# One product with B and one scan for two slots at a time on VectorE, with the states made in place

## The chip, the cores and the metric

The kernel runs on one core of a Trainium2 chip. The metric is the time of one execution on the device in microseconds (us). Smaller is better.

## What is computed

The input `x` is a batch of 16 images of 48 channels and 64x64 pixels, float32. Two layers follow one another. Each has a mixing step and a small feed-forward network, both added to the running `x`. The first layer mixes with a 3x3 depthwise convolution of one of four experts; the second with a two-dimensional cosine transform, after which each quarter of the spectrum goes through a selective state-space block ("mamba"), and an inverse transform. The change touches only the recurrence in that block:

```python
delta = softplus(einsum('blr,dr->bld', dt, dt_w) + dt_b)
A = -exp(A_log)
dA = exp(delta[..., None] * A)
dBu = delta[..., None] * Bm[:, :, None, :] * xi[..., None]
def step(h, inp):
    dA_t, dBu_t, C_t = inp
    h = dA_t * h + dBu_t
    return (h, einsum('bds,bs->bd', h, C_t))
h0 = zeros((B, d_inner, D_STATE))
_, ys = scan(step, h0, (dA, dBu, Cm))       # over L = 1024 positions
```

There are 96 inner channels with 16 states each, so 1536 recurrences of length 1024 for every image and quarter.

## The kernel before, in words

The 16 images go two at a time through `pair(p)`, eight times. A pair has 8 **units** (2 images times 4 quarters, `UNITS`), and a unit has 12 **slots** (`G`): a slot holds 8 channels x 16 states on the 128 partitions, and 1024 positions along the row (`L`). So there are 96 slots in a pair and 768 in the run. The stretch of a pair in which they are worked off is called the scan stage here. `scan_stage` walks through units `v` and slots `m` on every engine; each engine has its own program in that order, and they meet only at semaphores.

What is done for one slot, by engine:

- **SyncE** spreads 8 rows of delta from memory over the 128 partitions into `dbc` (line 461; a ring of 3).
- **ScalarE** makes the decay `da = exp(delta * A)` from it (`decay`, line 1240; a ring of `DAS` = 3 slots). It may overwrite a ring slot when the scan three slots back is done.
- **TensorE** spreads delta times input over the states with four matmul records (`broadcast_u`, lines 834 and 836) into two PSUM banks: banks 2 and 3 for even slots, 4 and 5 for odd ones. It may write a pair of banks when the scan two slots back is done (`h_ready`), because that scan still read them. In program order it stands one slot ahead of VectorE.
- **VectorE** multiplies these banks in place in PSUM by B (`step`, line 1571; this is called the product with B), and then runs the recurrence along the row (line 1576; this is called the scan). The scan reads the decay from the arena in SBUF and the product from PSUM, and writes the states to `hs` in the arena, a ring of `HSS` = 6 slots. `y_acc` says when a ring slot is free.
- **GpSimd** (POOL in the profile) multiplies the states by C, in place in `hs`, both inputs in SBUF (line 1680). Once in a unit it also makes the input of the next unit (line 1667), gates the output of the last one (line 1689), and adds a strip of the next pair's first layer (line 1697). It works in program order.
- **TensorE** sums three slots at a time over the states (`states`, line 857), which raises `y_acc`. Between these it does the projections of the next unit and the convolution of the next pair.

At the end of a stage VectorE makes the last product with C itself (line 1587, both inputs in SBUF).

Outside the scan stage, VectorE and GpSimd meet in the feed-forward stretches: there VectorE converts from SBUF to SBUF (line 1424, a CAST) while GpSimd adds (line 1638).

Everything named `arena` in the profile is one SBUF buffer; `da`, `hs`, `dbc`, B (`bmat`) and C (`cmat`) are parts of it. `ps` is PSUM.

Of the kernel before, what the change touches and what calls it, by code (L numbers as in the profile page):

```python
# [51 lines left out]
DAS = 3  # L52
HSS = 6
# [19 lines left out]
ARENA = 30300  # L73
# [5 lines left out]
def program(nc, a):  # L79
# [9 lines left out]
    with ctx:  # L89
# [43 lines left out]
        st = sb("st", [128, 8, ST])  # L133
        nrm = sb("nrm", [128, 6, ST + 2])
# [34 lines left out]
        yb = cut(R, 2 * CH // 2, F16).rearrange("p (b n) -> p b n", b=2)  # L169
        assert top[0] <= ARENA  # L170

# [94 lines left out]
        xs_zero = sem("xs_zero")  # L266
        xi_ps = sem("xi_ps")
# [124 lines left out]
        def scan_stage(prep, first, step, conv, last, early=lambda slot, v: None):  # L392
# [13 lines left out]
            last()  # L406

# [155 lines left out]
        def _(pe):  # L563
# [141 lines left out]
            def pair(p, last):  # L705
# [113 lines left out]
                def broadcast_u(v, m):  # L819
# [7 lines left out]
                    if v or m >= 2:  # L827
                        pe.wait_ge(h_ready, n - 1)
                    elif m == 0:
                        pe.wait_ge(sz_ready, 2 * p * UNITS + 2)  # L830
                    else:
                        pe.wait_ge(first_b, 2 * p + 2)
# [4 lines left out]
                              start=True, stop=True).then_inc(ubc_ready, 1)  # L837

# [9 lines left out]
                def states(v, r):  # L848
# [6 lines left out]
                    for c in range(2):  # L855
                        for b in range(TRIO):
                            mm = pe.matmul(ps[b * BLK:(b + 1) * BLK, c, :], gather[:, r, :],  # L857
                                           hs[:, (r * TRIO + b) % HSS, c * 512:(c + 1) * 512],
# [12 lines left out]
                def step(v, m):  # L871

                    w, k = after(v, m, 1)
                    if w < UNITS:
                        broadcast_u(w, k)
                    if v == 0 and m == 0:
                        states_first()
# [87 lines left out]
                scan_stage(prep, lambda: broadcast_u(0, 0), step, conv, final)  # L965
# [25 lines left out]
        def _(act):  # L991
# [102 lines left out]
            def rest(p, last):  # L1094
# [139 lines left out]
                def decay(v, m):  # L1234
# [5 lines left out]
                    act.activation(da[:, m % DAS, :], dbc[:, m % DBC, :], ACT.Exp,  # L1240
                                   scale=a_all[:, v // 2, m:m + 1]).then_inc(da_ready, 1)

                def first():
                    decay(0, 0)
                    for c in range(2):
                        first_states(c, 6 + c, first_c_ps, cmat, first_c)
                    for m in range(1, DAS - 1):
# [71 lines left out]
        def _(dve):  # L1319
# [223 lines left out]
            def rest(p, last, linked):  # L1543
# [16 lines left out]

                def step(v, m):
# [7 lines left out]
                    driven = two(2 + 2 * (m % 2))  # L1569
                    dve.wait_ge(ubc_ready, n + 1)  # L1570
                    dve.tensor_tensor(driven, driven, bmat[:, v % 2, :], ALU.mult).then_inc(bu_ready, 1)  # L1571
                    dve.wait_ge(bu_ready, n + 1)
                    dve.wait_ge(da_ready, n + 1)
                    if v or m >= HSS:
                        dve.wait_ge(y_acc, V * GPB + (m - HSS) // TRIO + 1)
                    dve.tensor_tensor_scan(hs[:, m % HSS, :], da[:, m % DAS, :], driven, 0.0,  # L1576
                                           ALU.mult, ALU.add).then_inc(h_ready, 1)
# [262 lines left out]
```

## Time and profile before

| | |
|---|---|
| median of 3 runs (lowest to highest) | 4236.63 us (4227.06 to 4249.97) |
| the execution that was profiled | 4219.27 us |
| its span in the trace | 4217.4 us |
| busy: TensorE, VectorE, ScalarE, GpSimd | 3708.7, 3493.2, 2772.9, 2345.8 us |
| scan stages, first product with B to line 1587 | eight of 337 to 343 us |

The profile is one execution, seen instruction by instruction. Busy time is the sum over an engine; the share of busy time is a mean over stages with different limits. A group of instructions is one line, operation and shape. "Idle before" is the time that the engine stood still just before these instructions, with what ended it. DVE is VectorE, ACT ScalarE, POOL GpSimd, PE TensorE, PEld its weight loads.

### The profile page before, as it was taken

How to read it: one execution, taken by the hardware profiler on the slowest of the kernel's cores; microseconds unless marked ns; L12 is line 12 of the kernel's file. 1: busy time of each engine (PE TensorE's matmuls, PEld its weight loads, DVE VectorE, ACT ScalarE, POOL GpSimd, SP SyncE). 2: the span in 40 equal slices, each digit the busy share in tenths (PEclk: the TensorE clock that was granted, in tenths of full speed). 3: DMA queues.
4: the chain of work that ended last, by engine and by line, in shares of the span. 5: the costliest groups of instructions: out<-in, count | busy, mean ns of one | idle time of the engine just before them, and what ended most of it. 6: DMA issues, size and time to landing. Idle time of an engine off the chain costs nothing.

```text
span 4217.4 us, 41720 instructions
## 1 busy us (share of the span) xinstructions
PE 3708.7 (88%) x14008; PEld 1348.4 (32%) x14008; DVE 3493.2 (83%) x3101; ACT 2772.9 (66%) x3212; POOL 2345.8 (56%) x1092
## 2 busy tenths in 40 slices
PE   6889988899879998899988999889988899878887
PEld 2332234222342223422244222432234322342223
DVE  2379987799778997699976999679987799778997
ACT  2567757777576775677666775767657767576764
POOL 0138762578426874177732787238762477426873
PEclk9999999999999999999999999999999999998878
DMA  1158861698518884288724887268961698507881
GB/s 40 35 144 214 214 166 47 169 220 205 134 51 207 206 220 100 72 215 219 206 63 119 214 209 171 75 146 212 217 167 47 165 220 201 141 18 196 199 204 46
DMA packets 186045, 644.72 MB, mean 153 GB/s; under 512 B 25660, under 2 KB 26600, under 8 KB 182280
## 3 DMA queue, kind: packets, MB, share of 16 engines
q1 hardware_dynamic: 168808, 596.95, 57.9%
q10 hardware_dynamic: 17024, 45.10, 3.5%
q8 instruction: 113, 1.85, 0.2%
q14 instruction: 100, 0.82, 0.1%
HBM read 525.40 MB, written 78.82 MB: 143 GB/s over the span
## 4 chain that ended last, share of the span: by engine, by line
DVE 35%; issue 25%; PE 18%; ACT 13%; DMA 4%; POOL 4%; SPq 0%; DVEq 0%; ACTq 0%; POOLq 0%
DVE ps L1571 15%; DVE arena L1576 13%; PE ps L673 4%; DMA arena<-dl 3%; PE ps L613 3%; PE ps L664 2%; ACT arena L1036 2%; ACT arena L1018 2%; POOL arena L1689 2%; POOL arena L1680 2%; ACT arena L1240 2%; PE ps L692 2%; DVE arena L1424 1%; ACT L1152 1%; ACT arena L1029 1%
## 5 line engine op out<-in xcount | busy, mean ns | idle before, releaser
L1680 POOL TENSOR_TENSOR arena<-arena 128x1024 f32<-128x1024 f32 x760 | 1785.9, 2359 | 704.3 <-DVE arena L1576 704.3
L1576 DVE TENSOR_TENSOR_SCAN arena<-arena,ps 128x1024 f32<-128x1024 f32 x768 | 1756.4, 2287 | 74.6 <-issue 31.6
L1240 ACT ACTIVATE arena<-arena,a_all 128x1024 f32<-128x1024 f32 x768 | 869.8, 1146 | 692.1 <-DMA arena<-dl 541.4
L834 PE MATMUL ps<-arena,spread 32*128 32x512 f32 x1536 | 876.4, 652 | 142.7 <-DVE arena L1576 140.9
L1571 DVE TENSOR_TENSOR ps<-ps,arena 128x1024 f32<-128x1024 f32 x768 | 928.3, 1209 | 57.5 <-PE ps L836 57.2
L836 PE MATMUL ps<-arena,spread 32*128 32x512 f32 x1536 | 869.1, 653 | 0.0
L857 PE MATMUL ps<-arena,gather 128*32 128x512 f32 x3072 | 519.4, 629 | 12.5 <-DVE arena L1587 12.4
L928 PE MATMUL ps<-x 96*96 96x512 f32 x1008 | 499.1, 613 | 26.5 <-ACT arena L1171 26.5
L834 PEld LDWEIGHTS ps<-arena,spread 32*128 32x128 f32 x1536 | 230.1, 186 | 785.9 <-DVE arena L1576 482.8
L1638 POOL TENSOR_TENSOR x<-x,arena 96x512 f32<-96x512 f32 x64 | 113.9, 1780 | 377.1 <-DVE arena L1415 377.1
L993 ACT ACT_TABLE_LOAD x226 | 290.0, 1283 | 24.7 <-DMA wo<-in_wo 20.7
L928 PEld LDWEIGHTS ps<-x 96*96 96x96 f32 x1008 | 142.3, 162 | 350.7 <-issue 350.7
L746 PE MATMUL ps<-arena,w_in 96*96 96x512 f32 x512 | 246.6, 609 | 8.0 <-ACT x L1286 7.8
L613 PE MATMUL ps<-arena,average 96*96 96x512 f32 x400 | 220.7, 634 | 30.7 <-ACT arena L1029 30.3
L1018 ACT ACTIVATE arena<-ps,eps 96x512 f32<-96x512 f32 x200 | 136.7, 684 | 144.3 <-PE ps L613 144.2
L857 PEld LDWEIGHTS ps<-arena,gather 128*32 128x32 f32 x3072 | 104.9, 112 | 384.8 <-issue 299.3
L836 PEld LDWEIGHTS ps<-arena,spread 32*128 32x128 f32 x1536 | 226.7, 186 | 0.0
L1657 POOL MEMSET arena<- 96x6 f32 x8 | 0.8, 103 | 388.3 <-DVE xq L1538 388.3
L1384 DVE TENSOR_TENSOR arena<-ps,arena 96x512 fp8e5<-96x512 f32 x128 | 86.9, 679 | 130.7 <-ACT arena L1023 130.1
L1036 ACT ACTIVATE arena<-ps 128x1536 f16<-128x1536 f32 x128 | 183.7, 1436 | 1.6 <-PE ps L632 1.6
L1638 POOL TENSOR_TENSOR x<-col_all,arena 96x512 f32<-96x512 f32 x64 | 103.6, 1619 | 145.9 <-DVE arena L1415 145.9
L643 PE MATMUL ps<-arena,w 128*96 128x512 fp8e5 x384 | 105.4, 384 | 83.4 <-DVE arena L1376 77.6
(160 smaller groups left out, 4907.8 us busy)
## 6 DMA issues: line engine op xcount, KB each, us to landing
arena<-dl SPq DMA_DIRECT2D x880, 512.0 KB, 6.9
dl<-arena ACTq DMA_DIRECT2D x64, 384.0 KB, 5.9
x<-pn SPq DMA_DIRECT2D x56, 247.5 KB, 10.5
arena<-in_x SPq DMA_DIRECT2D x9, 1536.0 KB, 13.2
arena<-xq SPq DMA_DIRECT2D x64, 192.0 KB, 6.2
arena<-arena ACTq DMA_DIRECT2D x64, 192.0 KB, 7.5
out<-x SPq DMA_DIRECT2D x64, 192.0 KB, 2.1
arena<-xq SPq DMA_DIRECT2D x64, 191.8 KB, 5.5
```

The lines of the kernel that those rows point to most:

```text
L613: pe.matmul(ps[0:R, LN_DEPTH + j % LN_DEPTH, :], average[:], sq[:, j % LN_DEPTH, :], start=True, stop=True).then_inc(averaged, 1)
L746: mm = pe.matmul(ps[0:DI, 6 + c, :], w_in[:, q, j, :], xs[:, i, c * 512 + 2 * j:c * 512 + 2 * j + 512], start=(j == 0), stop=(j == 1))
L834: pe.matmul(ps[:, bank, :], spread[rows[0], r, :], u[rows[0], i, 0:512], start=True, stop=True)
L836: pe.matmul(ps[:, bank + 1, :], spread[rows[1], r, :], u_low[rows[1], i, :], start=True, stop=True).then_inc(ubc_ready, 1)
L857: mm = pe.matmul(ps[b * BLK:(b + 1) * BLK, c, :], gather[:, r, :], hs[:, (r * TRIO + b) % HSS, c * 512:(c + 1) * 512], start=False, stop=( ...
L928: mm = pe.matmul(ps[0:R, 7, :], diag[:, k, :], taps_of(win[:, v % 2], k), start=(k == 0), stop=(k == TAPS - 1), skip_group_check=True)
L993: exp_table = lambda: act.preload_act_table_set("natural_log_exp_and_others")
L1036: act.activation(hf[:, j % 2, :], ps[:, 4:7, :].rearrange("p b n -> p (b n)"), ACT.Copy).then_inc(hf_ready, 1)
L1240: act.activation(da[:, m % DAS, :], dbc[:, m % DBC, :], ACT.Exp, scale=a_all[:, v // 2, m:m + 1]).then_inc(da_ready, 1)
L1571: dve.tensor_tensor(driven, driven, bmat[:, v % 2, :], ALU.mult).then_inc(bu_ready, 1)
L1576: dve.tensor_tensor_scan(hs[:, m % HSS, :], da[:, m % DAS, :], driven, 0.0, ALU.mult, ALU.add).then_inc(h_ready, 1)
L1680: pool.tensor_tensor(product, product, cmat[:, v % 2, :], ALU.mult).then_inc(pr_ready, 1)
```

## The change

VectorE now takes two slots in one instruction. The product with B reads four PSUM banks and writes to two ring slots of `hs`; the scan then reads decay and product, both from the arena, and writes the states over the product. The two slots are one row of 2048 to the scan; so that nothing of the first slot's last state goes into the second, the first decay of each slot is zero, and is written once in a pair by GpSimd: the exponentials then cover positions 1 to 1023. The first two slots of a stage and the last two are still done one at a time. `DAS` goes from 3 to 4, `HSS` from 6 to 8, and two small tables move into the arena, which grows by 1970 columns.

TensorE fills the four banks for two slots together, and no longer waits for the scan (`h_ready`) but for the product with B (`bu_ready`), since the product is what reads PSUM last.

```diff
-DAS = 3
-HSS = 6
+DAS = 4
+HSS = 8
...
+        def one_slot(v, m):
+
+            return (v == 0 and m < 2) or (v == UNITS - 1 and m >= G - 2)
...
                     if v or m >= 2:
-                        pe.wait_ge(h_ready, n - 1)
+                        pe.wait_ge(bu_ready, n - m % 2)
...
+                def first():
+
+                    broadcast_u(0, 0)
+                    broadcast_u(0, 1)
+                    states_first()
...
-                    w, k = after(v, m, 1)
-                    if w < UNITS:
+                    w, k = after(v, m, 2)
+                    if m % 2 == 0 and w < UNITS:
                         broadcast_u(w, k)
-                    if v == 0 and m == 0:
-                        states_first()
+                        broadcast_u(w, k + 1)
...
-                    act.activation(da[:, m % DAS, :], dbc[:, m % DBC, :], ACT.Exp,
+                    act.activation(da[:, m % DAS, 1:L], dbc[:, m % DBC, 1:L], ACT.Exp,
...
+                def scan(v, m, count):
+
+                    V = p * UNITS + v
+                    n = V * G + m
+                    h, d, b = (v * G + m) % HSS, m % DAS, 2 + 2 * (m % 2)
+                    driven = ps[:, b:b + 2 * count, :].rearrange("p (s b) n -> p s (b n)", s=count)
+                    state = hs[:, h:h + count, :]
+                    dve.wait_ge(ubc_ready, n + count)
+                    if v or m + count > HSS:
+                        dve.wait_ge(y_acc, V * GPB + (m + count - 1 - HSS) // TRIO + 1)
+                    dve.tensor_tensor(state, driven,
+                                      bmat[:, v % 2, :].rearrange("p (o n) -> p o n", o=1)
+                                      .broadcast_to([128, count, L]), ALU.mult).then_inc(bu_ready, count)
+                    dve.wait_ge(bu_ready, n + count)
+                    if v == 0 and m == 0:
+                        dve.wait_ge(da_zero, p + 1)
+                    dve.wait_ge(da_ready, n + count)
+                    line = state.rearrange("p s n -> p (s n)")
+                    dve.tensor_tensor_scan(line, da[:, d:d + count, :].rearrange("p s n -> p (s n)"), line, 0.0,
+                                           ALU.mult, ALU.add).then_inc(h_ready, count)
...
-                    driven = two(2 + 2 * (m % 2))
-                    dve.wait_ge(ubc_ready, n + 1)
-                    dve.tensor_tensor(driven, driven, bmat[:, v % 2, :], ALU.mult).then_inc(bu_ready, 1)
-                    dve.wait_ge(bu_ready, n + 1)
-                    dve.wait_ge(da_ready, n + 1)
-                    if v or m >= HSS:
-                        dve.wait_ge(y_acc, V * GPB + (m - HSS) // TRIO + 1)
-                    dve.tensor_tensor_scan(hs[:, m % HSS, :], da[:, m % DAS, :], driven, 0.0,
-                                           ALU.mult, ALU.add).then_inc(h_ready, 1)
+                    if one_slot(v, m) or m % 2 == 0:
+                        scan(v, m, 1 if one_slot(v, m) else 2)
...
                 pool.memset(xs[:, :, 0:PADL], 0.0).then_inc(xs_zero, 1)
+                pool.memset(da[:, :, 0:1], 0.0).then_inc(da_zero, 1)
```

VectorE at the start of a scan stage, in the order of the program. The scan stands there as SCALAR_TENSOR_TENSOR; `arena<-arena,ps` is out from in, and the brackets name the semaphores that it waits for. Before:

```order
L1571 TENSOR_TENSOR ps<-ps,arena 128x1024 [waits ubc_ready,first_b]
L1576 SCALAR_TENSOR_TENSOR arena<-arena,ps 128x1024 [waits da_ready,bu_ready]
L1571 TENSOR_TENSOR ps<-ps,arena 128x1024 [waits ubc_ready]
L1576 SCALAR_TENSOR_TENSOR arena<-arena,ps 128x1024 [waits da_ready,bu_ready]
L1571 TENSOR_TENSOR ps<-ps,arena 128x1024 [waits ubc_ready]
L1576 SCALAR_TENSOR_TENSOR arena<-arena,ps 128x1024 [waits da_ready,bu_ready]
L1571 TENSOR_TENSOR ps<-ps,arena 128x1024 [waits ubc_ready]
L1576 SCALAR_TENSOR_TENSOR arena<-arena,ps 128x1024 [waits da_ready,bu_ready]
```

The same place on VectorE now, slots 0 to 5:

```order
L1582 TENSOR_TENSOR arena<-ps,arena 128x1024 [waits ubc_ready,first_b]
L1590 SCALAR_TENSOR_TENSOR arena<-arena 128x1024 [waits da_ready,da_zero,bu_ready]
L1582 TENSOR_TENSOR arena<-ps,arena 128x1024 [waits ubc_ready]
L1590 SCALAR_TENSOR_TENSOR arena<-arena 128x1024 [waits da_ready,bu_ready]
L1582 TENSOR_TENSOR arena<-ps,arena 128x2048 [waits ubc_ready]
L1590 SCALAR_TENSOR_TENSOR arena<-arena 128x2048 [waits da_ready,bu_ready]
L1582 TENSOR_TENSOR arena<-ps,arena 128x2048 [waits ubc_ready]
L1590 SCALAR_TENSOR_TENSOR arena<-arena 128x2048 [waits da_ready,bu_ready]
```

From the third slot on there is one row of 2048 where there were two of 1024, and the scan's inputs are the arena alone.

TensorE in the first unit of a stage, around its slots 3 to 5 (L834 and L836 spread one slot, L857 sums three slots over the states, L759 is a projection, L928 the convolution). Before:

```order
L834 MATMUL ps<-arena,spread 128x512 [waits h_ready]
L836 MATMUL ps<-arena,spread 128x512
L759 MATMUL ps<-arena,w_dbc 128x512 [waits sz_ready] x2
L834 MATMUL ps<-arena,spread 128x512 [waits h_ready]
L836 MATMUL ps<-arena,spread 128x512
L857 MATMUL ps<-arena,gather 32x512 [waits pr_ready]
L857 MATMUL ps<-arena,gather 32x512 x5
```

The same place on TensorE now (L839 and L841 spread, L868 sums, L764 projects):

```order
L764 MATMUL ps<-arena,w_dbc 128x512 [waits sz_ready] x2
L839 MATMUL ps<-arena,spread 128x512 [waits bu_ready]
L841 MATMUL ps<-arena,spread 128x512
L839 MATMUL ps<-arena,spread 128x512 [waits bu_ready]
L841 MATMUL ps<-arena,spread 128x512
L868 MATMUL ps<-arena,gather 32x512 [waits pr_ready]
L868 MATMUL ps<-arena,gather 32x512 x5
```

Two slots are spread one behind the other, after the product with B of the two slots ahead of them and no longer after a scan; the other matmuls of two slots stand between.

## Rows read from the trace of the kernel before

**Rows 1.** The page, chain of work that ended last, shares of the span by engine.

```profile
DVE 35%; issue 25%; PE 18%; ACT 13%; DMA 4%; POOL 4%; SPq 0%; DVEq 0%; ACTq 0%; POOLq 0%
```

**Rows 2.** Eight scan stages: length, busy us (x instructions) by engine, granted clock, DMA.

```profile
core 0: us, PE busy (x) PEld busy (x) DVE busy (x) ACT busy (x) POOL busy (x), PEclk, DMA share, GB/s
263.30:606.30 343.00, 320.81 (x1132) 91.68 (x1130) 330.11 (x197) 238.11 (x234) 263.79 (x116) 0.99 0.82 202
...
3812.60:4149.90 337.30, 285.70 (x972) 77.67 (x970) 329.96 (x196) 208.56 (x203) 255.18 (x109) 0.84 0.80 192
sum 2728.00, PE 2519.23 PEld 717.20 DVE 2638.52 ACT 1875.14 POOL 2102.02; mean PE 314.90 PEld 89.65 DVE 329.82 ACT 234.39 POOL 262.75
```

**Rows 3.** Timeline of VectorE in a scan stage: start us, us, engine, line, operation.

```profile
338.16 1.21 DVE L1571 TENSOR_TENSOR ps<-ps,arena 128x1024 f32<-128x1024 f32 x1
339.40 2.29 DVE L1576 TENSOR_TENSOR_SCAN arena<-arena,ps 128x1024 f32<-128x1024 f32 x1
341.61 1.21 DVE L1571 TENSOR_TENSOR ps<-ps,arena 128x1024 f32<-128x1024 f32 x1
342.85 2.29 DVE L1576 TENSOR_TENSOR_SCAN arena<-arena,ps 128x1024 f32<-128x1024 f32 x1
```

**Rows 4.** VectorE by line and shape: count, busy us, mean ns, idle before.

```profile
L1576 DVE TENSOR_TENSOR_SCAN arena<-arena,ps 128x1024 f32<-128x1024 f32 x768 | 1756.4, 2287 | 74.6 <-issue 31.6 <-ACT arena L1240 10.3 <-DVE ps L1571 7.5
L1571 DVE TENSOR_TENSOR ps<-ps,arena 128x1024 f32<-128x1024 f32 x768 | 928.3, 1209 | 57.5 <-PE ps L836 57.2
...
L1609 DVE TENSOR_TENSOR x<-x,ps 96x512 f32<-96x512 f32 x64 | 43.7, 683 | 41.3 <-PE ps L673 40.4
...
L1587 DVE TENSOR_TENSOR arena<-arena 128x1024 f32<-128x1024 f32 x8 | 9.8, 1224 | 0.3
...
L1592 DVE TENSOR_TENSOR arena<-ps,arena 96x1024 f32<-96x1024 f32 x8 | 9.8, 1221 | 17.8 <-PE ps L857 17.8
```

**Rows 5.** One line each: duration ns min/median/max, first and last start.

```profile
L1576 DVE TENSOR_TENSOR_SCAN arena<-arena,ps x768: 2286/2287/2289, 265.9 to 4147.6; 128x1024 f32<-128x1024 f32 x192
...
L1680 POOL TENSOR_TENSOR arena<-arena x760: 2332/2357/2398, 268.3 to 4146.5; 128x1024 f32<-128x1024 f32 x190
```

**Rows 6.** Timeline of GpSimd in the same stage, with what ended its idle time.

```profile
320.52 6.97 POOL L1680 TENSOR_TENSOR arena<-arena 128x1024 f32<-128x1024 f32 x3
...
345.22 2.35 POOL L1680 TENSOR_TENSOR arena<-arena 128x1024 f32<-128x1024 f32 x1 [1.08 <-DVE arena L1576]
348.66 2.35 POOL L1680 TENSOR_TENSOR arena<-arena 128x1024 f32<-128x1024 f32 x1 [1.09 <-DVE arena L1576]
```

**Rows 7.** Timelines of VectorE and GpSimd at the ends of two scan stages.

```profile
606.28 1.22 DVE L1587 TENSOR_TENSOR arena<-arena 128x1024 f32<-128x1024 f32 x1
...
606.79 1.85 POOL L1697 TENSOR_TENSOR x<-x 96x512 f32<-96x512 f32 x1 [1.55 <-ACT x L1286]
...
1620.18 1.23 DVE L1587 TENSOR_TENSOR arena<-arena 128x1024 f32<-128x1024 f32 x1
...
1620.70 1.84 POOL L1697 TENSOR_TENSOR x<-x 96x512 f32<-96x512 f32 x1 [1.56 <-ACT x L1286]
...
L1697 POOL TENSOR_TENSOR x<-x x56: 1254/1269/1861, 319.3 to 3647.0; 96x512 f32<-96x512 f32 x56
```

**Rows 8.** Timelines in a feed-forward stretch, and the CAST's shortest, median and longest.

```profile
695.84 1.15 POOL L1638 TENSOR_TENSOR x<-col_all,arena 96x512 f32<-96x512 f32 x1 [1.90 <-DVE arena L1415]
...
696.00 1.81 DVE L1424 CAST arena<-arena 128x1536 fp8e5<-128x1536 f16 x1 [0.24 <-issue]
...
L1424 DVE CAST arena<-arena x128: 943/950/1824, 162.4 to 4209.4; 128x1536 fp8e5<-128x1536 f16 x128
```

**Rows 9.** Timeline of TensorE: one slot spread, and the next matmul behind it.

```profile
349.09 0.69 PE L834 MATMUL ps<-arena,spread 32*128 32x512 f32 x1
349.09 0.69 PE L836 MATMUL ps<-arena,spread 32*128 32x512 f32 x1
349.62 0.59 PE L834 MATMUL ps<-arena,spread 32*128 32x512 f32 x1
349.63 0.59 PE L836 MATMUL ps<-arena,spread 32*128 32x512 f32 x1
350.14 1.96 PE L746 MATMUL ps<-arena,w_in 96*96 96x512 f32 x4
```

More of the change, by code:

```diff
@@ L72 @@
 WIN = (ROWS + 2) * HP
-ARENA = 30300
+ARENA = 32270
 WS = KC + 3
@@ L132, in program @@
         pw_bias = sb("pw_bias", [R, 1])
-        st = sb("st", [128, 8, ST])
-        nrm = sb("nrm", [128, 6, ST + 2])
         x = sb("x", [R, PX])
@@ L169, in program @@
         yb = cut(R, 2 * CH // 2, F16).rearrange("p (b n) -> p b n", b=2)
+        st = cut(128, 8 * ST).rearrange("p (k s) -> p k s", k=8)
+        nrm = cut(128, 6 * (ST + 2)).rearrange("p (k s) -> p k s", k=6)
         assert top[0] <= ARENA
@@ L266, in program @@
         xs_zero = sem("xs_zero")
+        da_zero = sem("da_zero")
         xi_ps = sem("xi_ps")
@@ L857, in states @@
                             mm = pe.matmul(ps[b * BLK:(b + 1) * BLK, c, :], gather[:, r, :],
-                                           hs[:, (r * TRIO + b) % HSS, c * 512:(c + 1) * 512],
+                                           hs[:, (v * G + r * TRIO + b) % HSS, c * 512:(c + 1) * 512],
                                            start=False, stop=(r == GPB - 1), skip_group_check=True)
@@ L963, in final @@
                     project(QUADS - 1, 1, 7)
-                scan_stage(prep, lambda: broadcast_u(0, 0), step, conv, final)
+                scan_stage(prep, first, step, conv, final)
                 pe.wait_ge(mo_copied, (p + 1) * 2 * QUADS)
@@ L1244, in first @@
                     decay(0, 0)
+                    decay(0, 1)
                     for c in range(2):
                         first_states(c, 6 + c, first_c_ps, cmat, first_c)
-                    for m in range(1, DAS - 1):
+                    for m in range(2, DAS - 1):
                         decay(0, m)
@@ L1584, in final @@
                     n = V * G + G - 1
-                    q, i, slot = QUADS - 1, (UNITS - 1) % 2, (G - 1) % HSS
+                    q, i, slot = QUADS - 1, (UNITS - 1) % 2, (UNITS * G - 1) % HSS
                     dve.wait_ge(h_ready, n + 1)
@@ L1678, in step @@
                         pool.wait_ge(h_ready, n + 1)
-                        product = hs[:, m % HSS, :]
+                        product = hs[:, (v * G + m) % HSS, :]
                         pool.tensor_tensor(product, product, cmat[:, v % 2, :],
```

## The prediction, made before the changed kernel ran

> **What bounds the kernel now.** I read the shares of the chain of waits first [rows 1]: VectorE has 35% of it, more than any other engine. Shares over the whole run mix stages, so I read next the table of the eight scan stages [rows 2]. They take 2728 of 4217 us, and in each VectorE is busy for some 330 of 341 us, GpSimd for 264, ScalarE for 238. TensorE shows 321 us, but its records overlap. The timeline of VectorE [rows 3] shows how tight it is: product with B at 338.16, scan at 339.40, next product at 341.61, next scan at 342.85. That is 1.24 + 2.21 = 3.45 us a slot; 96 slots make 331 of the 341 us. So the scan stage is bound by VectorE issuing 2 instructions a slot without a gap, and the other 10 us are its waits [rows 4].
>
> Beside it GpSimd multiplies by C. A product takes 2.36 us, and GpSimd then stands still for 1.08 us until the next scan ends [rows 6]. It runs right through the scans and neither suffers: 768 scans lie between 2286 and 2289 ns, 760 products between 2332 and 2398 [rows 5]. What the two instructions read matters for what follows: the scan has one input in SBUF (the decay) and one in PSUM, GpSimd has both in SBUF.
>
> **The change on VectorE alone.** 92 of the 96 slots of a stage go in 46 instructions of two; 4 stay single. What it saves is the fixed part of an instruction. A product of 512 columns from PSUM to SBUF takes 683 ns, one of 1024 takes 1221 [rows 4], so 512 columns cost 538 and the fixed part is 145 ns. The new product also writes to SBUF, and 2048 columns should take 1221 + 1076 = 2.30 us against 2 x 1.21. For the scan there is one size only: between nothing and the 145 ns are saved, 4.57 or 4.43 us for two slots; I take 4.43, since it is the same engine. With the distances between starts that rows 3 show (0.03 us behind a product, -0.08 behind a scan), two slots go from 6.90 to 2.30 + 0.03 + 4.43 - 0.08 = 6.68 us. That would save 0.22 x 46 x 8 = 81 us.
>
> **The small parts.** GpSimd's extra memset and the new waits on it come once in a pair, in front of the first scan; the columns are four. The exponentials lose one column of 1024. TensorE must now spread two slots in a row, after the product with B. One takes 1.05 us from its start to the next matmul [rows 9], so two take 2.1, plus some 0.8 us until TensorE starts; the scan that runs meanwhile takes 4.43. If that cover were gone, up to 2.9 us a pair of slots would show. Queued behind TensorE's new wait are its sums over the states, its projections and the convolution; who waits for those (ScalarE, and VectorE through `y_acc`) stands two slots or more behind, and the ring has grown to 8. I count all of this at nothing.
>
> **The part that decides: the scan's second input.** The scan now reads its second input from SBUF too, and the trace shows what happens when VectorE and GpSimd both do that. At 606.28 VectorE starts its last product with C, line 1587, both inputs in SBUF. At 606.79, in the middle of it, GpSimd starts line 1697, and takes 1.85 us where its median is 1.27: 0.58 too long, so that it seems to begin at 607.37, 0.13 before VectorE ends at 607.50. At 1620.70 the same again, 1.84 us [rows 7]. The other way round it holds too: GpSimd adds from 695.84 for 1.15 us, undisturbed, and a CAST that VectorE starts at 696.00 takes 1.81 us where the median is 0.95 [rows 8]; it loses 0.86 us and seems to begin 0.13 us before GpSimd ends. So whoever comes second stands still until 0.13 us before the end of the first. Against it stands that line 1587 is a TENSOR_TENSOR and the CAST has one input; no scan with two inputs in SBUF is in the trace.
>
> The Trainium skill has this as a rule ("SBUF — State Buffer", section "Who interferes with whom"): a VectorE instruction with two SBUF inputs reads the second through an interface that it shares with GpSimd, and whichever of the two starts first keeps it for the whole instruction. Rows 7 and 8 agree; for a scan no run here shows it. By that rule the sum is the one that follows, without it the 81 us gain above.
>
> **The sum, if scans and GpSimd exclude each other.** Then neither VectorE's nor GpSimd's chain sets a stage, but both in turn: all of GpSimd's work plus all scans, while the products with B (one SBUF input) run beside GpSimd. Between two scans GpSimd needs 2 x 2.33 us (three in a row took 6.97 [rows 6]), the product with B only 2.30, so it is hidden. For each of the first seven stages:
> - GpSimd's work, by its busy time: 263.8 us [rows 2] (95 products with C, seven each of the three others).
> - Scans: 46 x 4.43 + 4 x 2.29 = 212.9.
> - Hand-over from GpSimd to VectorE, 0.13 us early: -0.13 x 50 = -6.5. The other way I take zero: it could be 0.13 early too, or 0.08 late, as GpSimd starts at 345.22 behind a scan that ended at 345.14 [rows 3, 6].
> - The first product with B, in front of everything: +1.2.
>
> That is 471.4 us where they now take (2728.0 - 337.3) / 7 = 341.5: +129.9 each, +909 for seven. The last stage has 255.2 us on GpSimd: 462.8 against 337.3, +125. Together +1034 us, and 4219.3 + 1034 = 5253. Whether VectorE or GpSimd wins a hand-over hardly matters: if scans go first, GpSimd falls behind, until TensorE's sums (which stand in front of the spreading of later slots) hold VectorE back and GpSimd catches up; one of the two is at work all the time. The saved 0.22 us is in the scans' 4.43, the product's part is hidden.
>
> TensorE stays below that: 321 / 48 = 6.7 us of work for two slots in 9.8. In the last stage its granted clock is 0.84, a mix of the levels of 2.4 and 1.2 GHz, with less to do, and the stage is no longer for it [rows 2]; at that mean 6.7 would be 8.0, still below 9.8.
>
> **Bounds of this case.** Both hand-overs 0.13 early: 50 x 0.13 x 8 = 52 less, 5200. GpSimd always 0.08 late, +32, and one wait of the size of the 1.55 us in rows 7 in each of 64 units, +99: 5380.
>
> The sum is against the profiled execution of 4219.3 us, which is 17 us below the median of the runs, inside their spread. I leave the forecast at **5250 us**.
>
> **Rivals.**
> - *No exclusion for scans* (10%). A scan takes 2.2 ns a column, twice a product [rows 4], so its inputs are read at half the rate, and GpSimd might find room between. Against it: the hold-up in rows 7 goes to the end of the instruction, not by shares. Then the 81 us are in reach: 4138. But TensorE's 6.7 us for two slots are then as long as VectorE's 6.68, and it waits for the product with B, so part of it may go again: 4140 to 4210. This is the case on the other side. It decides itself at a product with C of 2.36 us under a scan.
> - *Half a share* (6%). GpSimd runs at half speed under a scan, which isn't held up itself. Two slots bring GpSimd 263.8 / 48 = 5.50 us of work; 2.2 of it are done in a scan's 4.43, the other 3.3 behind it: 7.7 us against 341.5 / 48 = 7.1, 0.6 x 384 = 230 more, 4450. For it speaks only that nothing of the kind is in the trace.
> - *The change doesn't do what it says*: in the program the long instructions stand in pairs as told, so under 1%.
> - *Exclusion, with a further loss* (4%): TensorE at the lower clock for whole stages would need 13.4 us for two slots, above 9.8. That would be 3.6 x 384 = 1380 more. The last stage speaks against it.
>
> **Numbers.** Forecast 80%, its own span 5200 to 5380. The range must hold 8 in 10; I widen it to 5100 and 5440, since the price of a hand-over is known from a few rows only. Chances, with 0.5% (21 us) as what a measurement can tell from no change: faster 0.08, same 0.03, slower 0.89.
>
> **What would show it.** Right: GpSimd's products with C, or the scans of 2048 columns, last 4 to 7 us in part, with starts that fall on ends of the other engine; scan stages of 460 to 480 us; VectorE's recorded time in scans grows or GpSimd's does, though the work is the same; between two starts of a scan in mid-unit 8.9 to 9.9 us. The step on the fixed part is right if the product with B lasts 2.28 to 2.32 us, and the shortest scan 4.40 to 4.45. Wrong: products at 2.36 us under scans of 4.43, and stages below 345 us. If the exclusion shows but the time is above 5450, look at TensorE's granted clock in the scan stages and at waits for line 839.

## The result, and the profile after

The changed kernel takes 5206.85 us (median of 4 runs, 5206.24 to 5208.79), the kernel before 4232.12 us (4 runs, 4227.06 to 4249.97). The ratio is 1.2295, with a 95% interval of 1.2256 to 1.2333. The forecast was 5250, its range 5100 to 5440: the sign, the place and the mechanism came as told, and the forecast was 43 us too high. The execution that was profiled took 5207.17 us, with a span of 5205.4.

The page shows where the time went. Groups of instructions: line, operation, count, busy us, mean ns of one, idle time before them and what ended it. First three of the changed kernel, then GpSimd's product with C in the kernel before.

```profile
L1706 POOL TENSOR_TENSOR arena<-arena 128x1024 f32<-128x1024 f32 x760 | 2909.2, 3856 | 575.5 <-DVE arena L1590 376.3
L1590 DVE TENSOR_TENSOR_SCAN arena<-arena 128x2048 f32<-128x2048 f32 (+1 forms) x400 | 2687.5, 6719 | 60.0 <-ACT arena L1250 25.6
...
L1582 DVE TENSOR_TENSOR arena<-ps,arena 128x2048 f32<-128x2048 f32 (+1 forms) x400 | 872.0, 2180 | 112.9 <-PE ps L841 79.3
```

```profile
L1680 POOL TENSOR_TENSOR arena<-arena 128x1024 f32<-128x1024 f32 x760 | 1785.9, 2359 | 704.3 <-DVE arena L1576 704.3
```

L1706 is GpSimd's product with C. It is the same instruction as L1680 before, the same 760 times, but now takes 3856 ns in the mean; [rows 5] had none above 2398. The scan, L1590, has about half as many instructions and yet 2687.5 us where it had 1756.4 [rows 4]. Only the product with B, L1582, became cheaper, as a longer instruction should. So the two large groups that read twice from SBUF grew, by 1123 and 931 us. The other groups on these two engines that grew by more than 2 us read twice from SBUF as well: GpSimd's input for the next unit (L1693, 132.2 to 193.7 us) and its strip (L1723, 74.0 to 85.2), and VectorE's last product with C (L1612, 9.8 to 25.5). One line each, with the shortest, median and longest in ns:

```profile
L1590 DVE TENSOR_TENSOR_SCAN arena<-arena x400: 2290/6478/10001, 264.9 to 5130.8; 128x2048 f32<-128x2048 f32 x122, 128x1024 f32<-128x1024 f32 x12
...
L1706 POOL TENSOR_TENSOR arena<-arena x760: 2328/2360/6528, 268.1 to 5136.0; 128x1024 f32<-128x1024 f32 x190
...
L1582 DVE TENSOR_TENSOR arena<-ps,arena x400: 1191/2258/2293, 262.3 to 5129.5; 128x2048 f32<-128x2048 f32 x122, 128x1024 f32<-128x1024 f32 x12
```

GpSimd's median is untouched, its maximum is 4.1 us longer: most products run as ever, and some lose nearly all of a scan. Now the timeline in the middle of a stage: start, duration, engine, line. VectorE first, then GpSimd (x2 is two in a row, from the start of the first to the end of the second; the first of the two is the row above it).

```profile
434.22 2.26 DVE L1582 TENSOR_TENSOR arena<-ps,arena 128x2048 f32<-128x2048 f32 x1
436.57 4.45 DVE L1590 TENSOR_TENSOR_SCAN arena<-arena 128x2048 f32<-128x2048 f32 x1
440.94 2.26 DVE L1582 TENSOR_TENSOR arena<-ps,arena 128x2048 f32<-128x2048 f32 x1
443.29 6.48 DVE L1590 TENSOR_TENSOR_SCAN arena<-arena 128x2048 f32<-128x2048 f32 x1
449.69 2.26 DVE L1582 TENSOR_TENSOR arena<-ps,arena 128x2048 f32<-128x2048 f32 x1
452.04 10.00 DVE L1590 TENSOR_TENSOR_SCAN arena<-arena 128x2048 f32<-128x2048 f32 x1
```

```profile
434.38 2.36 POOL L1706 TENSOR_TENSOR arena<-arena 128x1024 f32<-128x1024 f32 x1 [4.36 <-DVE arena L1590]
...
436.70 6.47 POOL L1706 TENSOR_TENSOR arena<-arena 128x1024 f32<-128x1024 f32 x1
...
436.70 8.79 POOL L1706 TENSOR_TENSOR arena<-arena 128x1024 f32<-128x1024 f32 x2
```

Read the two side by side. A product with C is at work from 434.38 to 436.74. The scan that starts at 436.57 lasts only 0.03 us more than its undisturbed 4.42 (the run without reads below), so it begins to work at 436.60, 0.14 before the product ends. The next product starts at 436.70, behind that, and takes 6.47: it ends at 443.17, and without its own 2.36 it began at 440.81, 0.21 before the scan ended at 441.02. The product behind that runs from about 443.13 to 445.49 at its usual 2.36, and the scan issued at 443.29 takes 6.48: it works from 445.35, again 0.14 before the product's end. Two slots take 8.75 us here (436.60 to 445.35), where [rows 3] gives 6.90. The 10.00 us scan at the end waits out a gating, a strip and a product in the same way.

Now the stage as a whole, the row that answers to [rows 2]: window, length, busy us and count of TensorE, its weight loads, VectorE, ScalarE and GpSimd, granted clock, DMA share, GB/s. They are the first stage and the last, each to within 2 us.

```profile
262.30:725.30 463.00, 355.81 (x1127) 104.69 (x1126) 446.61 (x105) 238.39 (x233) 406.91 (x115) 0.83 0.60 150
4681.20:5132.00 450.80, 305.01 (x961) 85.61 (x958) 418.58 (x104) 207.30 (x203) 407.19 (x108) 0.74 0.59 144
```

VectorE's and GpSimd's busy times add up to 853 us in a stage of 461. They wait for each other while the profile calls them busy, which is why a busy share says so little here. By the starts and ends in the trace, the stages take 461.2, 461.4, 460.6, 462.8, 462.7, 460.8, 460.9 and 452.0 us (from the start of the first product with B to that of VectorE's last product with C, L1612, as in [rows 2]); together 3682.5 against 2727.9 before, +955. From its first scan on, each of them has only 1.6 to 2.0 us in which neither a scan nor one of GpSimd's instructions is on record; ahead of that scan stand the first product and a wait, 2.1 to 3.0 us.

The other +33 us lie behind the stages, 4 for each. Here is the end of the first: VectorE, then GpSimd's last two products.

```profile
723.52 3.19 DVE L1612 TENSOR_TENSOR arena<-arena 128x1024 f32<-128x1024 f32 x1
731.63 1.22 DVE L1617 TENSOR_TENSOR arena<-ps,arena 96x1024 f32<-96x1024 f32 x1 [4.92 <-PE ps L868]
```

```profile
721.30 4.33 POOL L1706 TENSOR_TENSOR arena<-arena 128x1024 f32<-128x1024 f32 x1
...
725.60 3.33 POOL L1706 TENSOR_TENSOR arena<-arena 128x1024 f32<-128x1024 f32 x1
```

Before, VectorE's last product with C took 1224 ns [rows 4] and GpSimd was long done. Now two of GpSimd's products are still to be done when line 1612 is issued: one ends at 725.63, so that it worked from 723.27, the other at 728.93, and between them VectorE has its 1.22 us, stretched to 3.19. TensorE's last sums wait for the second, and line 1617 for the sums: 4.92 us, where it waited 17.8 / 8 = 2.2 [rows 4].

### The profile page after: what moved, and what is told of

Read it like the earlier page. It is cut to its first block and busy times, and to the rows that moved or that the text cites. A ratio compares the mean times of both kernels' runs of the same rounds, so it can differ in the third digit from the quotient of the medians.

```text
span 5205.4 us, 41000 instructions
## 1 busy us (share of the span) xinstructions
PE 4004.8 (77%) x14008; PEld 1455.2 (28%) x14008; DVE 4417.4 (85%) x2365; ACT 2775.1 (53%) x3212; POOL 3541.7 (68%) x1100
## 5 line engine op out<-in xcount | busy, mean ns | idle before, releaser
L1706 POOL TENSOR_TENSOR arena<-arena 128x1024 f32<-128x1024 f32 x760 | 2909.2, 3856 | 575.5 <-DVE arena L1590 376.3
L1590 DVE TENSOR_TENSOR_SCAN arena<-arena 128x2048 f32<-128x2048 f32 (+1 forms) x400 | 2687.5, 6719 | 60.0 <-ACT arena L1250 25.6
L1250 ACT ACTIVATE arena<-arena,a_all 128x1023 f32<-128x1023 f32 x768 | 867.2, 1143 | 952.9 <-DVE arena L1590 722.5
L868 PE MATMUL ps<-arena,gather 128*32 128x512 f32 x3072 | 735.0, 856 | 624.1 <-POOL arena L1706 614.4
L1582 DVE TENSOR_TENSOR arena<-ps,arena 128x2048 f32<-128x2048 f32 (+1 forms) x400 | 872.0, 2180 | 112.9 <-PE ps L841 79.3
L839 PE MATMUL ps<-arena,spread 32*128 32x512 f32 x1536 | 792.0, 722 | 174.7 <-DVE arena L1582 171.9
L841 PE MATMUL ps<-arena,spread 32*128 32x512 f32 x1536 | 519.9, 755 | 0.0
L839 PEld LDWEIGHTS ps<-arena,spread 32*128 32x128 f32 x1536 | 250.2, 214 | 733.2 <-issue 492.9
L868 PEld LDWEIGHTS ps<-arena,gather 128*32 128x32 f32 x3072 | 128.1, 136 | 1115.2 <-POOL arena L1706 722.6
L764 PE MATMUL ps<-arena,w_dbc 96*128 96x512 f32 (+1 forms) x256 | 176.9, 826 | 96.8 <-ACT arena L1156 96.8
L1265 ACT ACTIVATE col_all<-ps 128x512 f32<-128x512 f32 x56 | 59.0, 1054 | 282.6 <-PE ps L877 282.4
L1693 POOL TENSOR_TENSOR arena<-arena 96x1024 f32<-96x1024 f32 x56 | 193.7, 3458 | 0.0
```

The lines of the kernel that those rows point to most:

```text
L839: pe.matmul(ps[:, bank, :], spread[rows[0], r, :], u[rows[0], i, 0:512], start=True, stop=True)
L841: pe.matmul(ps[:, bank + 1, :], spread[rows[1], r, :], u_low[rows[1], i, :], start=True, stop=True).then_inc(ubc_ready, 1)
L1250: act.activation(da[:, m % DAS, 1:L], dbc[:, m % DBC, 1:L], ACT.Exp, scale=a_all[:, v // 2, m:m + 1]).then_inc(da_ready, 1)
L1582: dve.tensor_tensor(state, driven, bmat[:, v % 2, :].rearrange("p (o n) -> p o n", o=1) .broadcast_to([128, count, L]), ALU.mult).then_inc ...
L1590: dve.tensor_tensor_scan(line, da[:, d:d + count, :].rearrange("p s n -> p (s n)"), line, 0.0, ALU.mult, ALU.add).then_inc(h_ready, count)
L1706: pool.tensor_tensor(product, product, cmat[:, v % 2, :], ALU.mult).then_inc(pr_ready, 1)
```

## The experiments

The theory is that scan and GpSimd exclude each other because the scan's second input moved to SBUF. The first rival is that something else in the change costs the time: the instructions of 2048 columns, the pairs on TensorE, or the deeper rings. The second is that they share the reads by parts instead of excluding each other.

### The part alone: states made in place, slots still one at a time

From the kernel before, with nothing but the product's target and the scan's second input changed (the wait for a free ring slot goes ahead of the product, since this now writes there):

```diff
+                    state = hs[:, m % HSS, :]
...
-                    dve.tensor_tensor(driven, driven, bmat[:, v % 2, :], ALU.mult).then_inc(bu_ready, 1)
+                    dve.tensor_tensor(state, driven, bmat[:, v % 2, :], ALU.mult).then_inc(bu_ready, 1)
...
-                    dve.tensor_tensor_scan(hs[:, m % HSS, :], da[:, m % DAS, :], driven, 0.0,
+                    dve.tensor_tensor_scan(state, da[:, m % DAS, :], state, 0.0,
```

> The kernel before with one part of the change alone: the product with B goes to the ring of states in SBUF, and the scan reads it from there and works in place. Everything stays single (1024 columns), rings, waits of TensorE and decays are as before. Theory (scans with two inputs in SBUF and GpSimd's reads exclude each other): a scan stage is GpSimd's 264 us plus 96 x 2.29 = 220 us of scans, less some 0.31 us for each of 96 hand-overs (what the changed kernel's stages of 461 us come to against 264 + 213), so some 454 us in place of 341, and 5100 to 5250 us in all. Scans and products with C last up to 2.3 us longer than alone. Rival (the loss comes from the long instructions or from TensorE's new order of two slots): the time stays between 4220 and 4300 us, with scans of 2.29 us.

It took 5322.32 us in one run, beside 4230.88 for the kernel before. No longer instruction, no deeper ring, no pair on TensorE, and all of the loss is there, even 115 us more of it than in the changed kernel. The scan (L1577) and the product with C (L1681) by line:

```profile
L1577 DVE TENSOR_TENSOR_SCAN arena<-arena x768: 2291/3436/5478, 266.2 to 5249.7; 128x1024 f32<-128x1024 f32 x192
...
L1681 POOL TENSOR_TENSOR arena<-arena x760: 2331/2355/4370, 268.7 to 5248.7; 128x1024 f32<-128x1024 f32 x190
```

The size was above my 5100 to 5250, and the timeline tells why. VectorE, then GpSimd:

```profile
409.25 3.43 DVE L1577 TENSOR_TENSOR_SCAN arena<-arena 128x1024 f32<-128x1024 f32 x1
...
413.83 5.45 DVE L1577 TENSOR_TENSOR_SCAN arena<-arena 128x1024 f32<-128x1024 f32 x1
419.20 1.19 DVE L1574 TENSOR_TENSOR arena<-ps,arena 128x1024 f32<-128x1024 f32 x1
420.42 3.43 DVE L1577 TENSOR_TENSOR_SCAN arena<-arena 128x1024 f32<-128x1024 f32 x1
```

```profile
414.79 2.34 POOL L1681 TENSOR_TENSOR arena<-arena 128x1024 f32<-128x1024 f32 x1
419.35 2.35 POOL L1681 TENSOR_TENSOR arena<-arena 128x1024 f32<-128x1024 f32 x1 [2.23 <-DVE arena L1577]
423.93 2.36 POOL L1681 TENSOR_TENSOR arena<-arena 128x1024 f32<-128x1024 f32 x1 [2.23 <-DVE arena L1577]
```

GpSimd has no old work here. It waits for the very scan that keeps it out, since it needs its states (2.23 us idle), and starts 0.07 us after its end: the scan at 413.83 ends at 419.28, the product starts at 419.35. So that hand-over is late instead of 0.2 early, and only the other one saves 0.14 (the product ends at 417.13, the scan works from 416.99). A slot takes 4.58 us (419.35 to 423.93). I had taken off 0.31 us a slot, and 0.07 is there; the missing 0.24 us, 96 times, make 23 us, and the first stage took 476.8 us instead of 454. In the changed kernel GpSimd lags by some slots and mostly has a product ready, so that it is issued under the scan and goes on 0.2 early. That, and the scans' own time (768 x 2.29 us here, 1701.7 us for the long ones where nothing holds them up, 57 us less), is most of what the pairs give back.

### GpSimd reads for half as long

From the changed kernel, with the product with C on the first 512 columns:

```diff
-                        product = hs[:, (v * G + m) % HSS, :]
-                        pool.tensor_tensor(product, product, cmat[:, v % 2, :],
+                        product = hs[:, (v * G + m) % HSS, 0:L // 2]
+                        pool.tensor_tensor(product, product, cmat[:, v % 2, 0:L // 2],
```

> The changed kernel with GpSimd's product with C cut to the first 512 of 1024 columns (half of that product is left out). Theory: the loss goes with the time that GpSimd reads. A product falls from 2.36 to some 1.26 us, GpSimd's work in a stage from 264 to 159 us, and a stage to 159 + 213 - 15 = 357 us, so 4340 to 4420 us in all. Rival (every meeting of a scan and a product costs a fixed time, whatever the length): most of the loss stays, above 4900 us.

4441.62 us in one run (before: 4230.88), 22 us above my upper end. By line:

```profile
L1706 POOL TENSOR_TENSOR arena<-arena x760: 1254/1272/5409, 268.9 to 4370.4; 128x512 f32<-128x512 f32 x190
...
L1590 DVE TENSOR_TENSOR_SCAN arena<-arena x400: 2291/4652/6037, 265.6 to 4370.5; 128x2048 f32<-128x2048 f32 x122, 128x1024 f32<-128x1024 f32 x12
```

Seven stages take 368 to 378 us, where I had reckoned 357 with GpSimd's shorter time in the same sum. Most of the difference is a wait that the sum doesn't have: scans stand 73.9 us for their decay (ScalarE, line 1250), 9 us a stage. So 765 us of the loss go when GpSimd reads for half the time, with the long instructions, the pairs and the rings all still there. The maximum of 5409 ns is again one product and the whole of a scan, 1.27 + 4.42 less a hand-over; at half speed, the "half a share" rival, a product of 1.27 us couldn't come to more than 2.5.

### GpSimd writes, but does not read

From the changed kernel, with the product with C turned into a memset of the same 1024 columns:

```diff
-                        pool.tensor_tensor(product, product, cmat[:, v % 2, :],
-                                           ALU.mult).then_inc(pr_ready, 1)
+                        pool.memset(product, 0.0).then_inc(pr_ready, 1)
```

> The changed kernel with GpSimd's product with C replaced by a memset of the same 1024 columns (the product with C is left out): GpSimd still writes SBUF at the same places, but reads nothing there. Its other three instructions of a unit still read. Theory (it is the reads that exclude each other): memsets keep one duration under scans and beside them, scans of 2048 columns last 4.42 to 4.45 us except where one of the other three instructions meets them, and the time falls to 4130 to 4260 us. Rival (any GpSimd access excludes a scan with two SBUF inputs): memsets or scans are stretched to the other's end, in both directions.

4332.19 us in one run (before: 4230.88). By line, then the groups of the page:

```profile
L1706 POOL MEMSET arena<- x760: 942/952/967, 269.2 to 4261.0; 128x1024 f32 x190
...
L1590 DVE TENSOR_TENSOR_SCAN arena<-arena x400: 2291/4425/5860, 266.2 to 4262.1; 128x2048 f32<-128x2048 f32 x122, 128x1024 f32<-128x1024 f32 x12
```

```profile
L1590 DVE TENSOR_TENSOR_SCAN arena<-arena 128x2048 f32<-128x2048 f32 (+1 forms) x400 | 1753.3, 4383 | 133.1 <-ACT arena L1250 102.1
...
L1582 DVE TENSOR_TENSOR arena<-ps,arena 128x2048 f32<-128x2048 f32 (+1 forms) x400 | 874.7, 2187 | 139.1 <-PE ps L841 82.5
```

On the question itself the answer is clean: 760 memsets between 942 and 967 ns, none held up, and scans at a median of 4425. The 55 scans that last longer all overlap one of the three instructions of GpSimd that still read (lines 1693, 1714 and 1722 of this kernel). The Trainium skill says it this way ("SBUF — State Buffer", section "Who interferes with whom"): a VectorE instruction with two SBUF inputs contends with a GpSimd instruction that reads SBUF and not with one that only writes it. These numbers agree.

The time was missed all the same; it is 72 us above my upper end of 4260. Beside the run that follows, which is 95 us faster, the two groups account for it: the scans have 52 us more (1753.3 - 1701.7, the readers that are left), the products with B 66 us more idle time (139.1 - 73.3), and the scans 19 less (133.1 - 151.9). Why TensorE is later here I didn't follow up.

### No reads at all, in both kernels

In the changed kernel and in the kernel before, the four instructions of GpSimd in the scan stage became memsets:

```diff
-                        pool.tensor_tensor(product, product, cmat[:, v % 2, :],
-                                           ALU.mult).then_inc(pr_ready, 1)
+                        pool.memset(product[:, 0:1], 0.0).then_inc(pr_ready, 1)
...
-                        pool.tensor_tensor(u[:, i, :], delta, xi[:, i, :], ALU.mult).then_inc(u_ready, 1)
+                        pool.memset(u[:, i, :], 0.0).then_inc(u_ready, 1)
...
-                    pool.tensor_tensor(yz[:, v % 2, :], yz[:, v % 2, :], sz[:, v % 2, :],
-                                       ALU.mult).then_inc(yz_ready, 1)
+                    pool.memset(yz[:, v % 2, 0:1], 0.0).then_inc(yz_ready, 1)
...
-                    pool.tensor_tensor(xr[:, i, :], xr[:, i, :], pwb, ALU.add).then_inc(xm_ready, 1)
+                    pool.memset(xr[:, i, 0:1], 0.0).then_inc(xm_ready, 1)
```

> The changed kernel with all four GpSimd instructions of the scan stage replaced by memsets (of one column, of the input of the next unit in full): the product with C, the gate, the next unit's input and the strip of the first layer are left out. What is left is what the change does to VectorE and TensorE alone. Theory: two slots take 2.35 + 4.37 = 6.72 us (the undisturbed distances in the changed kernel's trace) in place of 6.89, 0.17 x 368 = 63 us, and the waits of the rows of before may shrink too: 4120 to 4170 us, 1 to 2.5% below the same kernel before without reads. Rival (TensorE, which waits for the product with B and then spreads two slots, holds VectorE): 4190 us or more, no faster than the kernel before.

> The kernel before with the same four GpSimd instructions replaced by memsets (the same parts left out). Theory: GpSimd was off the path, so the time stays within 0.5% of the kernel before, 4200 to 4240 us. If GpSimd held something up in the kernel before, it falls below 4200.

The changed kernel without these reads takes 4236.59 us (10 runs, 4229.94 to 4243.49), 1.0012 times the kernel before (0.9993 to 1.003); the kernel before without them 4227.36, 0.9986 times (0.9963 to 1.0009). So these instructions of GpSimd cost the kernel before nothing that can be measured, and the changed one 970 us (5206.85 - 4236.59), all but a few us of the loss. That half came as expected.

The other half didn't: I had expected 4120 to 4170, a gain from the longer instructions. Line, timeline and group of the scan in the changed kernel without reads:

```profile
L1590 DVE TENSOR_TENSOR_SCAN arena<-arena x400: 2291/4425/4427, 265.7 to 4165.3; 128x2048 f32<-128x2048 f32 x122, 128x1024 f32<-128x1024 f32 x12
```

```profile
404.57 2.27 DVE L1582 TENSOR_TENSOR arena<-ps,arena 128x2048 f32<-128x2048 f32 x1
406.93 4.42 DVE L1590 TENSOR_TENSOR_SCAN arena<-arena 128x2048 f32<-128x2048 f32 x1
411.27 2.27 DVE L1582 TENSOR_TENSOR arena<-ps,arena 128x2048 f32<-128x2048 f32 x1
416.05 4.42 DVE L1590 TENSOR_TENSOR_SCAN arena<-arena 128x2048 f32<-128x2048 f32 x1 [2.51 <-ACT arena L1250]
```

```profile
L1590 DVE TENSOR_TENSOR_SCAN arena<-arena 128x2048 f32<-128x2048 f32 (+1 forms) x400 | 1701.7, 4254 | 151.9 <-ACT arena L1250 121.5
```

The scan of two slots now takes 4.42 us every time (median 4425 ns, longest 4427), and two slots take 6.70 us (404.57 to 411.27) against 6.90: 0.20 saved, 74 us over 368 pairs. But once in nearly every unit the scan of slots 6 and 7 stands 1.4 to 2.8 us for the second of its two decays (with the first scans of the stages 57 waits, 121.5 us), where the kernel before lost 74.6 before all its scans [rows 4]. That is 77 us more, and the gain is gone. A scan of two slots needs both decays before it starts; one slot at a time, the second had a slot's time more.

### Is it the rings? Three kernels without pairs

The change also makes the rings deeper. From the kernel before, with the loop, the product and the scan as they were:

```diff
-DAS = 3
-HSS = 6
+DAS = 4
+HSS = 8
```

```diff
-DBC = 3
-DAS = 3
+DBC = 4
+DAS = 4
```

```diff
-DAS = 3
+DAS = 4
```

The first has both rings of the change, with the ring slot counted as `(v * G + m) % HSS`; the second has the deeper decay ring and a deeper ring of deltas (and one semaphore more); the third the deeper decay ring alone. In all three the two small tables move into the arena, as in the change.

> The kernel before with the change's rings alone: DAS 4 and HSS 8, the two small tables in the arena; single slots, product with B in PSUM. In each unit the scan of one slot waits some 1.0 us for its decay, 57 in a run, where ScalarE is busy with the next unit. Theory (a deeper ring of decays lets ScalarE run ahead): 20 to 60 us less, 4160 to 4200. Rival (ScalarE waits for the spread delta, whose ring of 3 is unchanged): within 10 us of the kernel before.

> The kernel before with rings of 4 for both the decays and the spread delta that they are made from (DAS 4, DBC 4, HSS as before), tables in the arena. Theory (both rings together let ScalarE make its decays before it turns to the next unit): up to 60 us less, 4150 to 4200 us, and the wait of some 1.0 us in each unit is gone. Rival (what ScalarE has to do between two decays there is longer than any slot's lead): within 10 us of the kernel before.

> The kernel before with one ring alone deeper: DAS 4 (HSS stays 6, DBC stays 3), tables in the arena. The kernel with DAS 4 and HSS 8 was 2.7% slower than the kernel before, the one with DAS 4 and DBC 4 was not. Theory (with four decays and three buffers of delta, ScalarE comes to a decay one slot earlier, stands waiting for its delta, and its other work, the copy of y among it, comes late behind it, so that TensorE spreads late): slower as with both rings, 4310 to 4370 us. Rival (the ring of 8 states is what costs): within 20 us of the kernel before.

| kernel | median us (runs) | ratio to before, 95% interval |
|---|---|---|
| `DAS` 4, `HSS` 8 | 4343.21 (4) | 1.0271, 1.0228 to 1.0315 |
| `DAS` 4 alone | 4355.38 (4) | 1.0286, 1.0236 to 1.0335 |
| `DAS` 4, `DBC` 4 | 4215.46 (10) | 0.9989, 0.9966 to 1.0012 |

A deeper ring that costs 2.8% I hadn't foreseen: for both rings of the change I had expected a gain of 20 to 60 us. Groups of the page: first the kernel with `DAS` 4 alone, then the kernel before (its L1571 stands in [rows 4]).

```profile
L1240 ACT ACTIVATE arena<-arena,a_all 128x1024 f32<-128x1024 f32 x768 | 875.6, 1147 | 738.5 <-DMA arena<-dl 652.6
L1571 DVE TENSOR_TENSOR ps<-ps,arena 128x1024 f32<-128x1024 f32 x768 | 931.1, 1212 | 200.8 <-PE ps L836 200.6
...
L746 PE MATMUL ps<-arena,w_in 96*96 96x512 f32 x512 | 281.7, 683 | 78.2 <-ACT x L1286 78.1
```

```profile
L1240 ACT ACTIVATE arena<-arena,a_all 128x1024 f32<-128x1024 f32 x768 | 869.8, 1146 | 692.1 <-DMA arena<-dl 541.4
...
L746 PE MATMUL ps<-arena,w_in 96*96 96x512 f32 x512 | 246.6, 609 | 8.0 <-ACT x L1286 7.8
```

The product with B now waits 200.6 us for TensorE where it waited 57.2, and that is the loss: +143 there, 38 less before the scans. Follow it back in the timeline of the kernel with `DAS` 4 alone, ScalarE, TensorE and VectorE:

```profile
441.13 1.15 ACT L1240 ACTIVATE arena<-arena,a_all 128x1024 f32<-128x1024 f32 x1 [3.11 <-DMA arena<-dl]
442.19 0.67 ACT L1286 ACTIVATE x<-ps,pw_bias 96x512 f32<-96x512 f32 x1
```

```profile
442.91 3.73 PE L746 MATMUL ps<-arena,w_in 96*96 96x512 f32 x4 [3.08 <-ACT x L1286]
446.57 1.22 PE L834 MATMUL ps<-arena,spread 32*128 32x512 f32 x1
```

```profile
448.69 1.23 DVE L1571 TENSOR_TENSOR ps<-ps,arena 128x1024 f32<-128x1024 f32 x1 [3.95 <-PE ps L836]
```

ScalarE may now make a decay a slot earlier, arrives at it before its delta has come from memory, and stands for 3.11 us. It works in program order, so the bias behind it (line 1286) is late. TensorE needs that bias for line 746 and stands for 3.08 us; the matmuls behind it last 1.22 us where [rows 9] has 0.69, the lower of its two clock levels, 1.2 instead of 2.4 GHz (granted clock 0.50 from 443.0 to 448.6 us, 1.00 in the stretch of [rows 9]), after the engine stood idle. So the spreading is late, and VectorE waits 3.95 us. In the kernel with the deeper ring of deltas ScalarE waits 346.3 us for deltas instead of 652.6, line 746 waits 2.7, and the loss is gone. It isn't a gain either: the interval of its ratio holds 1.

In the changed kernel I don't count this loss beside the other: by the 1.6 to 2.0 us above, scans and GpSimd leave no room for it in a stage. No run has the changed kernel with the shallower ring.

### No reads, and no late decay

To see whether the 74 us can be had once the decays are early, the changed kernel without reads got a ring of deltas of 4; the room for it came from the ring of states, back to 6.

```diff
-DBC = 3
+DBC = 4
-HSS = 8
+HSS = 6
```

> The changed kernel without GpSimd's reads in the scan stage (the same four instructions replaced by memsets), and with a ring of 4 for the spread delta (DBC 4; HSS goes back to 6 to fit). With DBC 3 that kernel was no faster than the kernel before: in each unit the scan of slots 6 and 7 waits 2.1 to 2.8 us for its second decay, where the kernel before waited 1.0. Theory (the saving of 0.17 us in two slots is there, and is eaten by decays that come late): with the deeper ring that wait shrinks below 1 us and the time falls to 4130 to 4190 us. Rival (there is nothing to be saved, or ScalarE's own work sets that wait): 4210 us or more.

4457.29 us (4 runs), 1.0532 times the kernel before (1.0492 to 1.0571). I had expected 4130 to 4190; it fell. The product with B by line, and what ended its idle time (us, times), then the scan's:

```profile
L1582 DVE TENSOR_TENSOR arena<-ps,arena x400: 1197/2291/2293, 261.3 to 4380.9; 128x2048 f32<-128x2048 f32 x122, 128x1024 f32<-128x1024 f32 x12
...
  PE ps L868: 340.2, 196
```

```profile
  ACT arena L1250: 10.5, 12
```

The late decays are gone (10.5 us left of 121.5), but the product with B, which in this change writes the states' ring, now waits 340.2 us for TensorE's sums to free a slot there. No run has both rings deeper, so whether the longer instructions would bring their 74 us without contention stays open.

## Why the prediction was right, point by point

**The mechanism.** Shown from three sides: moving the second input alone makes the loss (5322), halving GpSimd's reading time takes over three quarters of it away (4442), and removing the reads takes all of it away (4237). Writes don't matter (memsets at 942 to 967 ns). The step that carried the prediction, from a TENSOR_TENSOR and a CAST in [rows 7, 8] to a scan of which the trace had none, held in full: whoever comes second stands still, for up to the other's whole length.

**The sum.** Each of the first seven stages was to take 471.4 us and took 460.6 to 462.8; the last 462.8 and took 452.0. That is 79 us less in eight stages (1034 - 955), and the 33 us behind the stages, which I had taken at nothing, go the other way. 1034 - 79 + 33 = 988 us is what the two profiled executions differ by. The step that failed is one term of the sum, the **hand-over**. For the first stage, 263.8 + 212.9 + 1.2 - 461.2 = 16.7 us are missing from the works put end to end, where I had taken off 6.5. Some 4.5 of them aren't saved: they are GpSimd's last two products (2.1 us of one from 723.5 on, 2.36 of the other), which my sum had inside the stage and the kernel does behind it, and these are the 33 us. The other 12 are 0.24 us for each of 50 scans, where I had 0.13, and 0.11 x 50 x 8 = 44 us is the 46 us that the sum was off. The timeline shows where the rest comes from: 0.14 early from GpSimd to VectorE, as told, and up to 0.21 early the other way, which I had put at zero. For that I had [rows 6], where GpSimd waits for the scan itself. The run with in-place states alone shows that row's case, 0.07 late; in the changed kernel GpSimd lags and mostly has work waiting. Reckoned in this way for every change of turn in the eight stages (an end less the undisturbed duration), a scan goes on 0.14 us early in the median; GpSimd goes on 0.20 early where it was issued before the scan's end (302 times) and 0.08 late where it was not (98); together 0.25 us a scan. The lower bound that I gave for the hand-overs, 5200, is nearly the result.

**The fixed part.** The product with B of two slots takes 2.26 us (forecast 2.30; outside my 2.28 to 2.32 by a hair), so 0.16 us and not 0.145 is saved. The undisturbed scan takes 4.42 (forecast 4.43). A scan starts 0.09 us behind the product (404.57 + 2.27 against 406.93), not 0.03, so a pair of slots takes 6.70 us without contention, not 6.68. In the changed kernel the product's part of this is hidden.

**Starts of scans in mid-unit**, forecast 8.9 to 9.9 us apart: 461 / 48 = 9.6 in the mean, but the single distances are 8.75 where two products lie between, 6.72 where GpSimd is out of work (436.57 to 443.29), and more where the once-a-unit work comes in. The mean was right for a less even pattern than I had drawn.

**TensorE.** Its clock fell further than I had reckoned with, to 0.83 in the stage where it had 0.99, and 0.74 in the last. It costs next to nothing: from the first scan of a stage on, 1.6 to 2.0 us pass without a scan or GpSimd on record, so no more than that can be lost to TensorE there. The product with B waits 112.9 us in the run, twice as much as before, under cover of GpSimd.

**The rivals.** "Half a share" is out by the durations. "No exclusion" was wrong in its price too: at 4138 I had the 81 us and up to 72 of TensorE's waiting against them, and the run without reads stands at 4237. The late second decay, which took the gain there, I had not seen at all, though [rows 4] shows the scan waiting for line 1240.

## What to carry to other kernels

Before an operand of a VectorE instruction moves from PSUM to SBUF, count its SBUF inputs and look at what GpSimd reads at that time: two inputs on both sides made two engines here that had run side by side into one. The price can be worked out beforehand from any place in the trace where the two already meet, if one subtracts the usual duration from the long one and sees where the work really begins. And an instruction that covers two steps waits for the later of its inputs; the fixed cost that it saves (0.20 us for two slots) was used up here by one late input (1.4 to 2.8 us) in nearly every unit.

## What the runs showed of the hardware and the queues, not expected

- The hand-over isn't the same both ways: VectorE goes on 0.14 us before GpSimd's instruction ends, GpSimd some 0.20 before VectorE's scan ends, but only if it was issued beforehand. Issued by that scan's end, it starts 0.07 to 0.08 us late.
- A deeper ring alone made the kernel before 2.8% slower, since ScalarE then stood in its queue at an earlier wait (3.11 us) with work behind it that TensorE needed, and TensorE's matmuls went from 0.69 to 1.22 us after the idle time.
